# Fourier layers on one core: image-innermost spectra, a product on four 32-column tiles, early loads, and another order of transposes

## The reference

```python
h = einsum('bhwi,ic->bhwc', x, fc0_w) + fc0_b          # 3 -> 64 channels
for l in range(4):
    xf  = rfft2(h)
    top = einsum('bixy,ioxy->boxy', xf[:, :, :16, :16], w1[l])
    bot = einsum('bixy,ioxy->boxy', xf[:, :, -16:, :16], w2[l])
    sc  = irfft2(zero spectrum with top and bot set)
    y   = sc + einsum('bihw,oi->bohw', h, pw_w[l]) + pw_b[l]
    h   = gelu(batch norm of y over images and pixels)
```

## Time and profile before

| | us |
|---|---|
| median of 3 runs (lowest, highest) | 2792.32 (2785.29, 2792.57) |
| the profiled execution, its time | 2789.79 |
| the profiled execution, its span | 2788.0 |
| PE busy | 2315.3 |
| DVE busy | 1711.1 |
| ACT busy | 1753.7 |
| POOL busy | 192.5 |

### The profile page before, as it was taken

How to read it: one execution, slowest core, us unless ns; L and a number is a source line. 1 busy time by engine, 2 the same in 40 slices (tenths; PEclk the granted TensorE clock), 3 DMA queues, 4 the chain that set the end, 5 groups by cost and what they waited for, 6 DMA issues and landing times. The chain is left out here.

```text
span 2788.0 us, 75068 instructions
## 1 busy us (share of the span) xinstructions
PE 2315.3 (83%) x32251; PEld 1463.7 (53%) x32251; DVE 1711.1 (61%) x2617; ACT 1753.7 (63%) x2739; POOL 192.5 (7%) x237
## 2 busy tenths in 40 slices
PE   7569979965997997599979956996996577765999
PEld 4546646654664665566646655663221466633444
DVE  4657767765776776567767755775002877744443
ACT  2823357766776776767767775775996477722333
POOL 0000000000000000000000000000000233301443
PEclk9879989988999999899989988998998799976999
DMA  4645567646998873699977457997552000012342
GB/s 167 198 143 214 213 260 241 213 145 207 361 349 293 283 239 108 190 341 350 351 273 237 158 175 244 362 356 279 194 178 65 1 1 1 1 26 50 89 92 58
DMA packets 179062, 537.18 MB, mean 193 GB/s; under 512 B 23183, under 2 KB 38223, under 8 KB 178511
## 3 DMA queue, kind: packets, MB, share of 16 engines
q1 hardware_dynamic: 178735, 532.38, 57.0%
HBM read 362.57 MB, written 170.37 MB: 191 GB/s over the span
## 5 line engine op out<-in xcount | busy, mean ns | idle before, releaser
L395 PE MATMUL P<-cst,mem 128*128 128x128 f32 (+1 forms) x3760 | 560.4, 286 | 75.2 <-ACT mem L658 26.3
L395 PEld LDWEIGHTS P<-cst,mem 128*128 128x128 f32 (+1 forms) x3760 | 408.3, 143 | 245.7 <-issue 191.3
L640 ACT ACTIVATE mem<-P,small 128x512 f32<-128x512 f32 x512 | 323.6, 684 | 331.5 <-PE P L502 245.4
L502 PEld LDWEIGHTS P<-cst,mem 64*128 64x128 f32 x4096 | 249.1, 187 | 207.9 <-DVE mem L778 110.9
L790 DVE BATCH_NORM_STATS2 mem<-mem 128x6 f32<-128x512 f32 x512 | 327.2, 681 | 35.4 <-ACT mem L640 35.2
L502 PE MATMUL P<-cst,mem 64*128 64x128 f32 x4096 | 298.5, 285 | 0.0
L820 DVE COPY mem<-P 128x512 f32<-128x512 f32 x384 | 246.8, 683 | 78.8 <-PE P L395 77.5
L630 ACT ACTIVATE mem<-mem,small 128x1024 f32<-128x1024 f32 x192 | 238.0, 1240 | 42.2 <-DMA mem<-z_d 42.2
L449 PE MATMUL P<-mem 128*64 128x64 f32 x4096 | 161.4, 252 | 114.5 <-issue 53.8
L778 DVE COPY mem<-P 128x512 f32<-128x512 f32 x256 | 176.6, 690 | 106.5 <-PE P L395 106.0
L783 DVE COPY mem<-P 128x512 f32<-128x512 f32 x256 | 174.8, 686 | 108.7 <-PE P L483 108.7
(11 more groups left out here) (168 smaller groups left out, 3162.1 us busy)
## 6 DMA issues: line engine op xcount, KB each, us to landing
mem<-z_d SPq DMA_DIRECT2D x384, 512.0 KB, 4.9
z_d<-mem SPq DMA_DIRECT2D x256, 512.0 KB, 6.5
mem<-in_wmix SPq DMA_DIRECT2D x64, 1024.0 KB, 8.6
G_d<-mem SPq DMA_DIRECT2D x128, 256.0 KB, 3.5
mem<-G_d SPq DMA_DIRECT2D x128, 256.0 KB, 5.7
hz<-z_d SPq DMA_DIRECT2D x64, 512.0 KB, 4.6
mdB<-dT_d SPq DMA_DIRECT2D x44, 384.0 KB, 5.6
mem<-in_x SPq DMA_DIRECT2D x128, 12.0 KB
```

The costliest lines, as they stand in the source:

```text
L395: return nc.tensor.matmul(out, in_, ident[0:n, 0:n], start=True, stop=True, is_transpose=True)
L502: last = nc.tensor.matmul(banks[x][:, j * 128:j * 128 + 128], ATs[o, a.q % 2, j * 128:j * 128 + 128], i2c[o, x * 128:x * 128 + 128], start ...
L640: nc.scalar.activation(ychunk(a, h), P[4 + 2 * (a.q % 2) + h][:, :], ACT.Identity, bias=bias0 if first else pwb_c).then_inc(S["eY"], 1)
```

## The change

- `XX` is laid out as ky, kx, image, images innermost (first in `mem`). A step's plain operand is now 1024 contiguous columns of `XX`, and TensorE takes its stationary operands of 32 columns directly from there. Only the swapped operand is written, by one instruction of VectorE and one of ScalarE a step, from contiguous columns to contiguous columns. L611 and L751 are gone.
- The spectrum's writers, L832 and L683 in the forward stage and L732 and L595 in layer 0, write one image's values with a stride of 32 values (one ky to the next: 512 values).
- The product runs on four tiles of 32 columns: 64 products per step instead of 32.
- Eight of the late weight rows go to the place of the forward stage's pixel ring, and their four loads wait for the last F1 instead of the last X.
- The first six quarters of the forward stage are loaded during the previous inverse stage's end; the first two quarters of the inverse stage are loaded behind the product's last stores (layers 1 to 3).
- In TensorE's forward step the order is T1, T2, X, F1, F2 instead of T1, F1, T2, F2, X.
- Parts of `mem` move accordingly.

```diff
-        XX = part(16384, 16384)
+        XX = part(0, 16384)
         def weights(ky):
-            if ky < W_EARLY:
-                return part(32768 + ky * 1024, 1024)
-            return part(8192 + (ky - W_EARLY) * 1024, 1024) if ky < W_EARLY + 8 else weights(ky - W_EARLY - 8)
+            a = W_EARLY + 8 if ky >= W_EARLY + 8 else 0
+            return 32768 + (ky - a) * 1024 if ky < W_EARLY or a else 23552 + (ky - W_EARLY) * 1024
...
+        zq = [part(23552 + i * 1024, 1024) for i in range(FR)]
+        SG = [16384 + i * 1024 for i in range(3)]
...
-        def operands(s):
-            return SG[s % 3].rearrange("p (b k v i) -> p v b k i", b=2, k=16, v=2)
-        def spectra(s):
-            return XX.rearrange("p (i k y) -> p y k i", k=16, y=KY)[:, 2 * s:2 * s + 2]
+        def swapped(s, r):
+            return mem[r * 64:r * 64 + 64, SG[s % 3]:SG[s % 3] + 1024]
+        def spectra(s, r):
+            return XX[r * 64:r * 64 + 64, s * 1024:s * 1024 + 1024]
+        def operand(s, m, v):
+            o = (SG[s % 3] if v else s * 1024) + m * 32
+            return mem[:, o:o + 32]
         def spectrum(r, image, q):
-            o = image * MODES + q * 256
-            return XX[r * 64:r * 64 + 64, o:o + 256].rearrange("p (i n) -> p i n", i=4)
+            return XX[r * 64:r * 64 + 64, :].rearrange("p (y a x i) -> p a x y i", y=KY, a=8, x=2)[:, q * 4:q * 4 + 4, :, :, image]
...
             def mix_loads(l):
...
-                    sp.wait_ge(S["pX"], l * 32)
+                    sp.wait_ge(S["pF1"], l * 64)
...
+                if l:
+                    sp.wait_ge(S["pM"], l * 32 + 24)
+                    for q in range(2):
+                        load_pixels(l, False, At(0, 0, q, 0))
...
             # inv_loads, step
-                    if a.ok:
+                    if a.ok and (first or a.s >= 2):
...
+                    if t == PAIRS // 2 and u == 0 and q < 2 and l + 1 < layers:
+                        for v in range(2):
+                            sp.wait_ge(yst[v], (l * 16 + 2) * 32)
+                        for s in range(3 * q, 3 * q + 3):
+                            load_quarter(s)
...
             # TensorE, mix
-                                o, k = b * 1024 + (2 * i + x) * 64, (8 * x + i) * 64
-                                last = nc.tensor.matmul(P[n % 8][x * 64:x * 64 + 64, i * 64:i * 64 + 64], SG[s % 3][:, o:o + 64], weights(n)[:, k:k + 64], start=True, stop=True)
+                                k = weights(n) + (8 * x + i) * 64
+                                for v in range(2):
+                                    j = (2 * x + v) * 32
+                                    last = nc.tensor.matmul(P[n % 8][j:j + 32, i * 64:i * 64 + 64], operand(s, b * 16 + 2 * i + x, v), mem[:, k:k + 64], start=True, stop=True)
...
             # ScalarE, mix (VectorE likewise: swapped(s, 0) from spectra(s, 1), times -1)
-                    nc.scalar.activation(operands(s)[64:128, 1], spectra(s)[0:64], ACT.Copy).then_inc(S["sgA"], 1)
-                    if s % 2 == 0:
-                        nc.scalar.activation(operands(s)[:, 0], spectra(s), ACT.Copy).then_inc(S["sgA"], 1)
+                    nc.scalar.activation(swapped(s, 1), spectra(s, 0), ACT.Copy).then_inc(S["sgA"], 1)
...
             # layer 0's spectrum (VectorE likewise)
-                    last = nc.scalar.activation(XX[0:64, m:m + MODES], P[2 * (b % 2)][o, :], ACT.Copy)
+                    last = nc.scalar.activation(XX[0:64, :].rearrange("p (m i) -> p m i", i=IMG)[:, :, m], P[2 * (b % 2)][o, :], ACT.Copy)
```

More of the change, by code:

```diff
@@ L95, in part @@
             return mem[:, off:off + n]
-        XX = part(16384, 16384)
+        XX = part(0, 16384)
         def weights(ky):
-            if ky < W_EARLY:
-                return part(32768 + ky * 1024, 1024)
-            return part(8192 + (ky - W_EARLY) * 1024, 1024) if ky < W_EARLY + 8 else weights(ky - W_EARLY - 8)
+            a = W_EARLY + 8 if ky >= W_EARLY + 8 else 0
+            return 32768 + (ky - a) * 1024 if ky < W_EARLY or a else 23552 + (ky - W_EARLY) * 1024
         def weight_rows(ky):
-            a = W_EARLY + 8 if ky >= W_EARLY + 8 else 0
-            off = 32768 + (ky - a) * 1024 if ky < W_EARLY or a else 8192 + (ky - W_EARLY) * 1024
-            return part(off, 2048).rearrange("p (w n) -> p w n", w=2)
+            return part(weights(ky), 2048).rearrange("p (w n) -> p w n", w=2)
@@ L113, in build_fno @@
         zbuf = [part(32768 + 6144 + i * 4096, 4096) for i in range(2)]
[L115 to L139, removed]
+        B0 = 16384
+        xall = mem[0:96, B0:B0 + 4096]
+        sel0 = mem[0:96, B0 + 4096:B0 + 6144]
@@ new lines, in build_fno @@
+        Xx = mem[0:96, B0 + 6144:B0 + 7168]
+        hT = [part(B0 + 8192, 1024), part(B0 + 9216, 1024)]
+        hT2 = [part(B0 + 10240, 512), part(B0 + 10752, 512)]
+        A1 = [part(B0 + 11264, 2048)]
+        Ax = [part(16384 + i * 2048, 2048) for i in range(2)]
+        AxT = part(20480, 2048)
+        Xy = part(22528, 1024)
+        zq = [part(23552 + i * 1024, 1024) for i in range(FR)]
+        hTq = [part(29696 + i * 1024, 1024) for i in range(2)]
+        SG = [16384 + i * 1024 for i in range(3)]
@@ L140, in build_fno @@
+        Gs = [part(20480 + i * 1024, 1024) for i in range(2)]
+        Ai = [part(0, 2048), part(2048, 2048)]
+        ybuf = [part(4096, 2048), part(6144, 2048)]
+        Gt = [part(8192, 1024), part(9216, 1024)]
+        ATs = part(10240, 1024).rearrange("p (s n) -> p s n", s=2)
+        stats = part(11264, 768)
         fc0b_c, pwb_c, gam_c, bet_c = (small[:, i:i + 1] for i in range(4))
@@ L525, in step @@
                             last.then_inc(S["pT1"], 1)
+                    a = At(t, u, q, 8)
+                    if a.ok:
+                        wait(pe, "eF1", b64 + a.pair * 4 + 4)
+                        wait(pe, "eT2", b64 + a.s)
+                        for i in range(4):
+                            o = (a.q * 4 + i) * 128
+                            last = tr(P[4][:, i * 128:i * 128 + 128], Ax[a.par][:, o:o + 128])
+                        last.then_inc(S["pT2"], 1)
+                    a = At(t, u, q, 14)
+                    if a.ok and a.q < 2:
+                        wait(pe, "eF2", b32 + a.pair * 2 + 2)
+                        if a.q == 0:
+                            wait(pe, "eXa", b16 + a.pair)
+                        else:
+                            wait(pe, "eXd", b16 + a.pair + 1)
+                        for i in range(4):
+                            k = a.q * 4 + i
+                            last = tr(P[7][:, i * 128:i * 128 + 128], Xy[:, k * 128:k * 128 + 128])
+                        last.then_inc(S["pX"], 1)
                     a = At(t, u, q, 3)
@@ L543, in step @@
                         last.then_inc(S["pF1"], 1)
-                    a = At(t, u, q, 8)
-                    if a.ok:
-                        wait(pe, "eF1", b64 + a.pair * 4 + 4)
-                        wait(pe, "eT2", b64 + a.s)
-                        for i in range(4):
-                            o = (a.q * 4 + i) * 128
-                            last = tr(P[4][:, i * 128:i * 128 + 128], Ax[a.par][:, o:o + 128])
-                        last.then_inc(S["pT2"], 1)
                     a = At(t, u, q, 9)
@@ L566, in step @@
                         last.then_inc(S["pF2"], 1)
-                    a = At(t, u, q, 14)
-                    if a.ok and a.q < 2:
-                        wait(pe, "eF2", b32 + a.pair * 2 + 2)
-                        if a.q == 0:
-                            wait(pe, "eXa", b16 + a.pair)
-                        else:
-                            wait(pe, "eXd", b16 + a.pair + 1)
-                        for i in range(4):
-                            k = a.q * 4 + i
-                            last = tr(P[7][:, i * 128:i * 128 + 128], Xy[:, k * 128:k * 128 + 128])
-                        last.then_inc(S["pX"], 1)
                 over_steps(pe, step, PAIRS // 2 + 2)
```

24 lines of the change are left out of this document (10 added, 14 removed).

## The result

The changed kernel takes 2795.81 us (median of 20 runs, 2791.55 to 2810.84) against 2788.06 for the kernel before (20 runs, 2781.46 to 2793.91): ratio 1.0029, 95% interval 1.0019 to 1.0040. The forecast was 2700, with a range of 2655 to 2750. The span of the profiled execution is 2791.7 us against 2788.0. Some parts gained, and others lost as much.

What follows compares the result with a forecast made beforehand. No engine was full over the span: ScalarE bounded the product, TensorE the forward stage, DMA and TensorE the inverse. Savings 53 + 15 + 4 + 25 - 3 - 4 = 90 took 2789.8 to 2699.8 us; range 2655 to 2750, own range 2675 to 2725.

Steps and rivals of the forecast that it cites:

- Operand copies: Product: L611 and L751 go, ScalarE's contiguous copy takes 1.15 us instead of 2.02; a step costs ScalarE 1.9.
- Four column tiles: Product: 128 records a step instead of 64, at 16 ns each 2.05 us; upper bound 4.0.
- the Trainium skill's rule of row groups: Product: weight loads overlap running products only in another row group, so a step would take 4.0 us, not 2.05.
- What is late next in the product: Product: the store ring sets the step at 2.9 us; stage 56.5 us against 70.5, 53 saved over four layers.
- the store ring: Product: evictions of step s+2 wait for step s's stores in two staging slots; 2.9 us a step, low bound 2.2.
- Rival A: Product: TensorE bounds it at 4.0 us a step, by tiles sharing the array or a 1.2 GHz clock; 2743, chance 0.10.
- Late weights: Forward stage's tail: four late weight loads issued after the last L542; worth 0 alone, lets the first stores land undelayed.
- Early loads: Pixels loaded in advance: forward start's 5.02 us wait goes, 15 saved; 4 saved by moving inverse loads under the hand-over.
- The start gains nothing: Hand-over: first inverse products wait for G_d anyway, so two early pixel quarters change nothing at the inverse start.
- the cover named for the six quarters among the y stores: Inverse end: with the inverse pixel loads over by then, early loads cost 0; without that, 3 a layer, -9.
- Transposes first: Forward stage: fewer switches and no wait for L832 cut the pair from 11.86 us to 10.76 at best.
- Strided writes: Spectrum writes: 0.16 us more per 256 values, 0.65 a pair on either engine; pair taken as 11.2 us, 25 saved.

Runs made afterwards that it cites:

- order-alone kernel: Kernel before with only TensorE's forward order changed (T2 and X ahead of F1 and F2), spectrum still written contiguously: 2743.92 us, ratio 0.9834.
- the two-tile version: Changed kernel with the product on two tiles of 64 columns and the plain half copied again from contiguous columns, ScalarE and VectorE in turns: 2747.17 us, ratio 0.9851.

## Why the prediction was wrong

1. *Operand copies*: right. ScalarE's copy takes 1.05 us for a forecast of 1.15, one for each engine and step.
2. *Four column tiles*: the price of a record was right, 128 in 1.99 us for 2.05. By the Trainium skill's rule of row groups, cited there, twice the loads would have cost twice the time, and this trace does not agree: 16 ns a record on four tiles of one row group, 30 on two. What was wrong is that the price of 128 records was taken for the price of a step.
3. *What is late next in the product*: the step that failed. It named the store ring, 2.9 us a step, and compared it with ScalarE and TensorE alone. Missing was the supply of instructions, which the sum puts at nothing without a reason: 3.67 us for 128 load and matmul pairs with no other traffic, 4.2 to 4.8 in the product. Doubling the records made it the longest of all, 4.2 to 4.8 us a step for the 2.9 of the ring. 53 us of gain became a loss of 6.5. Of these 60 us some 46, an estimate by the records' spread in all four products, lie above the quiet 3.67 a block. With half the records the ring and its size appear as forecast: 55.0 to 56.4 us in layers 1 to 3 for 56.5.

   The Trainium skill ("Runtime: NRT & Kernel Launch", section "Instruction fetch mechanics") describes the mechanism: each engine's sequencer brings its own instructions over a DMA queue in blocks of 16 KiB, 256 instructions. The packets agree. It calls the cost of crossing a block mostly hidden; here it is not, once 256 instructions take less than 3.67 us to run. The kernel's other stages stay away from it: the steady forward part runs 2026 matmuls in 130.5 us, 8.2 us for 128, the inverse 3296 in 180, 7.0.

   Rival A had nearly the right step (4.0 us) for another reason, and its 2743 still kept the other gains. Its clock of 1.2 GHz did occur, granted 0.50 from 1130 to 1135: blocks of 3.64 us, yet with 3.50 and 3.77 us of idle time before them.
4. *Late weights*: not tried by themselves.
5. *Early loads*: the start gained 12 of 15, since 0.90 of the 5.02 us is a wait that loads don't touch. "The start gains nothing" at the hand-over was optimistic: the pixel loads stand ahead of the first G_d load and delay its landing, 2.3 to 3.6 us in layers 1 to 3, 9 together. And the cover named for the six quarters among the y stores did not hold: the stage ends 1.3, 4.3 and 2.7 us later, 8.3 together, close to the 9 that stood there as the bound. Whether taking 1 MB out of the inverse stage gained the 4 us can't be told from its spread between layers and runs.
6. *Transposes first*: right. The pair takes 10.81 us for a best case of 10.76, and the order alone shortens the whole by 46 us.
7. *Strided writes*: the mechanism right, the size short. 0.18 us more for VectorE's 256 values (forecast 0.16), 0.24 for ScalarE's (0.16), by the means of L832 and L683 alone, 419 and 379 ns from 900 to 1070 in the order-alone kernel, against 605 and 623. The pair came to 11.40 for 11.2. Against 10.81 without them that is 0.59 a pair for 0.44, and 12.5 x 0.59 = 7.4 a layer; the stage lost 10.7, so by subtraction its first and last steps and the few longer pairs cost the other 3.3, 10 in three layers for the 3 forecast.

"No change" had a chance of 0.01, "if the parts cancel". They did: gains of 21 us against losses of 26. Each rival doubted one part; none put the doubts of three parts together.

## What to carry to other kernels

Count the instructions of an engine per microsecond as a bound of its own: on TensorE 128 weight loads with their matmuls came every 3.7 us on average with no other traffic, bursts of some 300 excepted, and up to 7.4 us apart where weight loads and stores filled the DMA engines. Splitting a product over twice as many tiles doubled the instructions; where such a product uses up blocks faster than they come, as here, the shorter records gain little. Loads issued ahead did better behind the last transfer that someone waits for than in front of it. And price a layout by both ends: contiguous reads in one stage were strided writes in another.

The best version found has two tiles, contiguous copies, four staging slots, the new order, and the early quarters behind the last store: 2698.34 us. It still writes the spectrum strided; the same with contiguous writes was not tried.

## What the runs showed of the hardware

- TensorE's instructions come in packets of 16 KB for 256 of them, one per 3.67 us on average while it uses them up and nothing else moves. At the end of a product, with 130 to 150 GB/s of other traffic, it is 3.67 to 3.68 too; with over 290 GB/s 6.2 to 7.4. Such a packet takes part of that time only (the queue's share is 1.8% of 16 engines); what fills the rest was not found.
- Records of 128 rows by 32 columns on four tiles with 64 moving columns take 16 ns each within a block, 128 by 64 on two tiles 30 ns, both at 2.4 GHz.
- A write of ScalarE from PSUM with a stride of 2 KB took 619 ns for 256 values against 378 contiguous, of VectorE 605 against 419. With 128 bytes and 512 values (layer 0) it was 1042 against 592 and 1031 against 690. Per value that is 0.9 ns more on ScalarE and 0.7 on VectorE at either stride. Reading SBUF with a stride of 2 KB cost as much: ScalarE's 1024 values took 2.02 us against 1.05, also in the two-tile version, which like the kernel before writes in runs of 32 values.
